# Mixture results returned to token order by row addresses, with a new order of norms and routes

## What is computed

```
# B, S, D = 2, 1024, 128; four blocks, each followed by a residual and a layernorm
x = _layernorm(x + attention(x))              # 16 heads of 64, q and k normalized
x = _layernorm(x + _moe_forward(x, ...))      # gate, top 2 of 8 experts
x = _layernorm(x + _L1_attn_ref(x, ...))      # depthwise convolution, then a recurrence
x = _layernorm(x + _L1_ffn_ref(x, ...))       # router, top 2 of 8 experts, one shared MLP
...
# first mixture, for the two chosen experts e of a token, weights by softmax of the two logits
hidden = silu(x_flat @ wge.T) * (x_flat @ wue.T);  out += we[:, None] * (hidden @ wde.T)
# recurrence, 16 states for each of 128 channels
dt = sigmoid(xf @ dt_w.T + dt_b) * (DT_MAX - DT_MIN) + DT_MIN
s = expA * s + (dtt * xt)[..., None] * b;  y = einsum('bcd,cd->bc', s, c)
# second mixture: two chosen experts, and the shared MLP for every token
_mlp(x) = square(relu(x @ w_fc.T)) @ w_proj.T
```

## Time and profile before

| | us |
|---|---|
| median of 3 runs | 1077.84 (1076.33 to 1078.65) |
| the profiled execution, its own time | 1075.24 |
| span of its profile | 1073.5 |

### The profile page before, as it was taken

One profiled execution on the slowest core, in us unless ns is written; L12 is line 12 of the kernel. 1 busy time (PEld: TensorE's weight loads), 2 busy tenths in 40 slices (PEclk: granted clock), 3 DMA queues, 4 the chain that ended last, 5 costly groups with the idle time before them and its releaser, 6 DMA issues. The chain is left out here.

```text
span 1073.5 us, 34731 instructions
## 1 busy us (share of the span) xinstructions
PE 913.9 (85%) x13676; PEld 858.4 (80%) x13676; DVE 728.1 (68%) x1463; ACT 770.0 (72%) x1275; POOL 501.1 (47%) x385
## 2 busy tenths in 40 slices
PE   4889999999999999999999951899969469899930
PEld 2778998999989989989999841899969359899830
DVE  6699988988998898889888744432459669410202
ACT  5689998988999889989988640544464266598831
POOL 5475755564655555555646116512328152043433
PEclk8799999999999999999999965899999689899975
DMA  8300000000000000000000041313201002023211
GB/s 263 113 2 6 18 3 22 3 3 22 3 3 22 3 22 3 3 23 3 2 22 2 2 177 38 103 54 86 54 26 30 3 28 70 11 68 97 61 55 42
DMA packets 43131, 42.13 MB, mean 39 GB/s; under 512 B 5600, under 2 KB 37344, under 8 KB 42848
## 3 DMA queue, kind: packets, MB, share of 16 engines
q1 hardware_dynamic: 38880, 31.51, 9.6%
q0 software_dynamic: 4096, 8.40, 2.7%
HBM read 25.60 MB, written 14.29 MB: 37 GB/s over the span
## 5 line engine op out<-in xcount | busy, mean ns | idle before, releaser
L557 ACT ACTIVATE Pr<-SC,cur_nesc,cur_esc 128x1024 f32<-128x1024 f32 x256 | 309.9, 1211 | 33.5 <-PE SC L417 17.0
L654 DVE TENSOR_TENSOR Pl<-Pr 128x1024 f16<-128x1024 f32 x224 | 287.5, 1302 | 44.8 <-ACT Pr L557 43.0
L416 PE MATMUL SC<-QK 128*128 128x256 f16 x1024 | 238.7, 274 | 1.0 <-ACT QK L539 1.0
L417 PE MATMUL SC<-QK 128*128 128x256 f16 x1024 | 238.6, 273 | 0.0
L442 PE MATMUL OP<-V,Pr 128*128 128x65 f16 x2048 | 214.4, 192 | 5.8 <-DVE Ob L676 5.7
L444 PE MATMUL OP<-V,Pr 128*128 128x64 f16 x2048 | 215.2, 195 | 0.0
L446 PE MATMUL OP<-V,Pl 128*128 128x65 f16 x2048 | 214.0, 191 | 0.0
L442 PEld LDWEIGHTS OP<-V,Pr 128*128 128x128 bf16 x2048 | 191.0, 97 | 12.5 <-issue 8.2
L444 PEld LDWEIGHTS OP<-V,Pr 128*128 128x128 bf16 x2048 | 190.0, 97 | 2.5
L446 PEld LDWEIGHTS OP<-V,Pl 128*128 128x128 f16 x2048 | 190.7, 99 | 0.0
L789 POOL TENSOR_TENSOR stk<-nrm,stk 128x512 f16<-128x512 f32 x64 | 75.2, 1175 | 147.6 <-DVE stk L636 147.6
(11 more groups left out here) (191 smaller groups left out, 2178.8 us busy)
## 6 DMA issues: line engine op xcount, KB each, us to landing
ys<-yb SPq DMA_DIRECT2D x92, 64.0 KB, 1.5
...
wd<-in_wd SPq DMA_DIRECT2D x4, 576.0 KB, 10.7
...
```

Source lines behind the costliest of these rows:

```text
L416: eng.matmul(out, QK[:, b, 1, key:key + P], rhs, start=True, stop=False)
L417: mm = eng.matmul(out, QK[:, b, 2, key:key + P], rhs, start=False, stop=True)
L557: eng.activation(Pr[:, n % PB, :, :], SC[s % 2][:, :, :], ACT.Exp, bias=cur_nesc[:, b:b + 1], scale=cur_esc[:, b:b + 1]).then_inc(s_exps, 1)
L654: eng.tensor_tensor(Pl[:, n % PB, :, :].rearrange("p a b -> p (a b)"), pr, high(pr)[:, 1::2], ALU.subtract).then_inc(s_low_probs, 1)
```

## The change

**Addresses.** A row of xs is now 288 f16 values long, 576 bytes. Behind the two halves stand the token's number plus 1024 and its first choice. xs and ys now exist once for each phase. At the start SP clears four tensors xs, not two, each with two DMAs, and the padding rows get addresses behind the results. When a chunk is loaded, two small DVE instructions (`return_addresses`) work out where each row's result belongs. The results go back by indirect DMA from POOL, one for each tile (`give_back`, 92 in all), straight to the place of token and choice. SP's 92 stores and POOL's 64 gathers are gone; SP reads a phase's results with four plain loads (`load_rows`). yb has 12 buffers.

**Waits.** `scatter` no longer waits for tiles: 16 DMAs go in a row. The third scatter stands ahead of phase 2's returns, the fourth behind the sixteenth return of phase 2.

**Order.** `place` follows `choose`, and ranks(0) stands ahead of logits(1). The norm, turn and convolution of batch 0 and its step products are spread over units 35 to 43, its tanh and first exponential stand at unit 45. The sums and the norm (1, 1) of phase 1 stand between the first 16 scans. The second batch's convolution is ahead of its route. Its states go through PE one per unit from unit 46, its last norm and turn are at units 64 and 65, the ranks at 69.

```diff
+        eng.wait_ge(self.s_zero, 4)
+        self.clear_rows(eng, range(B))
+
+    def clear_rows(self, eng, phases):
+        t = self.t
+        for ph in phases:
+            rows = t["xs"][ph].rearrange("(j p) c -> p j c", p=P)
+            eng.dma_start(rows[:, :, 0:2 * D],
+                          self.zero[:, :].unsqueeze(1).to_broadcast([P, TILES, 2 * D])).then_inc(self.s_cleared, 16)
+            eng.dma_start(rows[:, :, 2 * D:ROW], self.pad[:, :, :].bitcast(F16)).then_inc(self.s_cleared, 16)
...
                 eng.dma_start(wst[:, :], io["up0"][:, bass.ds(2 * FF * i, 2 * FF)]).then_inc(s_up_loaded, 16)
 
-            for i in range(H // 2):
+            load(0)
+            constants.sync(eng)
+            load(1)
+            constants.clear_rows(eng, range(B, 2 * B))
+            for i in range(2, H // 2):
                 load(i)
+            constants.sync_ended(eng)
 
...
 SORTED = TILES * P
+ROW = 2 * D + 32
+ADDRESS = slice(2 * D, 2 * D + 4)
 LAG2 = 2
...
-YR = 8
+YR = 12
...
+STEP_0 = CONVOLVE_0 + 1
 AHEAD = 10
-TURN_2 = SPARSE_2 + 5
+ROWS_2 = SPARSE_2 + 10
+TURN_2 = SPARSE_2 + 11
+RANKS_3 = TURN_2 + 4
 
 
 def states_behind(u):
 
-    n = AHEAD + 2 * (u - SPARSE_2)
-    return range(n, n + 2) if AHEAD <= n < DS else ()
+    n = AHEAD + u - SPARSE_2
+    return range(n, n + 1) if AHEAD <= n < DS else ()
 
 
 def sorted_tile(u):
...
                 wait(eng, s_sorted_turned, J - TILES + js.stop)
-                rows = xs[ph % 2].rearrange("(j p) c -> p j c", p=P)
+                wait(eng, s_dest, CHUNKS * (ph - 1) + c + 1)
+                rows = xs[ph].rearrange("(j p) c -> p j c", p=P)
                 eng.dma_start(xg[:, js, :], rows[:, js, :]).then_inc(s_sorted_loaded[c], 16)
 
-            def store(ph, j):
-                J = TILES * ph + j
-                eng.wait_ge(s_down_read, J + 1)
-                eng.dma_start(ys[ph % 2][P * j:P * j + P, :], yb[:, J % YR, :]).then_inc(s_y_stored[J % YR], 16)
+            def load_rows(ph, h):
+
+                for r in range(YR):
+                    wait(eng, s_y_stored[r], 16 * len(range(r, TILES * ph + TILES, YR)))
+                wait(eng, s_combined, 2 * TB * ph)
+                rows = ys[ph][0:2 * S].rearrange("(k i p) d -> p k i d", k=2, p=P)
+                for k in range(2):
+                    eng.dma_start(yg[:, k, 4 * h:4 * h + 4, :], rows[:, k, 4 * h:4 * h + 4, :]).then_inc(
+                        s_gathered[ph][h], 16)
 
             def store_out(b):
...
-                load(2, c)
-            for j in range(TILES):
-                store(2, j)
-            for c in range(CHUNKS):
-                load(3, c)
-            for j in range(TILES):
-                store(3, j)
+            for l in range(2):
+                for b in range(B):
+                    for c in range(CHUNKS):
+                        load(2 * l + b, c)
+                for b in range(B):
+                    for h in range(2):
+                        load_rows(2 * l + b, h)
             for b in range(B):
                 store_out(b)
             eng.wait_ge(s_out, 16 * 2 * B)
...
-                    turn(1, 0)
-            step_products(0)
+                if u in (TURN_1, TURN_1 + 1):
+                    turn(1, 0, (u - TURN_1,))
+                if u == STEP_0:
+                    step_products(0)
             for n in range(DS):
                 state_products(0, n)
+                if n == 12:
+                    turn(1, 1)
             turn(2, 0)
             logits(2)
-            turn(1, 1)
+            step_products(1)
             ranks(2)
             for u in range(SHARED_0, SPARSE_2 + LAG2):
                 if u < SPARSE_2:
                     up_products(u)
                 if u >= SHARED_0 + LAG2:
                     down_products(u - LAG2)
-                if u == STEP_1:
-                    step_products(1)
-                if u >= SPARSE_2 - 3:
...
-                if u == TURN_1:
-                    read(1, 0)
-            sigmoids(0)
-            for n in range(DS):
+                if u in (ROWS_1, ROWS_1 + 1):
+                    rows(1, 0, (u - ROWS_1,))
+                if u in (TURN_1, TURN_1 + 1):
+                    read(1, 0, (u - TURN_1,))
+                if u == SHARED_0 - 1:
+                    sigmoids(0)
+                    decays(0, 0)
+            for n in range(1, DS):
                 decays(0, n)
+                if n == 13:
+                    rows(1, 1)
+            read(1, 1)
             rows(2, 0)
             read(2, 0)
-            rows(1, 1)
-            read(1, 1)
             split_high(2)
             weights(2)
+            sigmoids(1)
+            decays(1, 0)
+            decays(1, 1)
             for u in range(SHARED_0, SPARSE_2):
                 activate(u)
...
@@ -1380,11 +1419,12 @@
                 for n in states_behind(u):
                     if n + NEA < DS:
                         decays(1, n + NEA)
+                if u == ROWS_2:
+                    rows(2, 1)
                 if u == TURN_2:
-                    rows(2, 1)
                     read(2, 1)
                     split_high(3)
-                if u == TURN_2 + 1:
+                if u == RANKS_3:
                     weights(3)
...
@@ -1498,6 +1539,19 @@
                 eng.tensor_tensor(w1l[m // 2][:, half], stage[:, n * m:n * m + n], w1h[m // 2][:, half],
                                   ALU.subtract).then_inc(s_w1_low, 1)
 
+            def return_addresses(ph, c):
+
+                b, js = ph % 2, chunk_tiles(c)
+                eng.wait_ge(s_sorted_loaded[c], 16 * ph + 16)
+                eng.tensor_tensor(is_first[:, js], sender[:, js, 1], owner[:, b, js], ALU.is_equal).then_inc(
+                    s_is_first, 1)
+                eng.wait_ge(s_is_first, CHUNKS * ph + c + 1)
+
+                wait(eng, s_y_stored[(TILES * (ph - 1) - 1) % YR],
+                     16 * len(range((TILES * (ph - 1) - 1) % YR, TILES * (ph - 1), YR)) if ph > 1 else 0)
+                eng.scalar_tensor_tensor(out=dest[:, b, js], in0=is_first[:, js], scalar=-float(S),
+                                         in1=sender[:, js, 0], op0=ALU.mult, op1=ALU.add).then_inc(s_dest, 1)
+
             def diagonal(n):
                 eng.tensor_scalar(diag[:, n, :], t["ident32"][:, :], t["bc"][:, n:n + 1], None, ALU.mult).then_inc(
                     s_diag, 1)
...
-                    statistics(1, 0, (0,))
-                if u == 40:
-                    combine(0, 1)
-                    statistics(1, 0, (1,))
-                if u == 41:
+                if u % TILES in RETURN_AT:
+                    return_addresses(u // TILES, RETURN_AT.index(u % TILES))
+                if u in (COMBINE_0, COMBINE_0 + 1):
+                    combine(0, u - COMBINE_0)
+                    statistics(1, 0, (u - COMBINE_0,))
+                if u == COMBINE_0 + 2:
                     shifts(1, 0)
-            convolve(0)
+                if u == CONVOLVE_0:
+                    convolve(0)
             step_inputs(0)
             for n in range(DS):
                 scan(0, n)
+                if n in (7, 9):
+                    combine(1, (n - 7) // 2)
+                    statistics(1, 1, ((n - 7) // 2,))
+                if n == 10:
+                    shifts(1, 1)
             add_states(0)
             statistics(2, 0)
-            combine(1, 0)
-            statistics(1, 1, (0,))
             shifts(2, 0)
-            combine(1, 1)
-            statistics(1, 1, (1,))
+            convolve(1)
+            split_low(2)
             choose(2)
-            shifts(1, 1)
             low(0)
-            split_low(2)
+            place(2)
             probabilities(2)
-            place(2)
-            convolve(1)
-            add_shared(SHARED_0)
-            add_shared(SHARED_0 + 1)
             step_inputs(1)
             for n in range(DS):
                 scan(1, n)
-                if n < TB - 2:
-                    add_shared(SHARED_0 + 2 + n)
+                if 0 <= n - 2 < TB:
+                    add_shared(SHARED_0 + n - 2)
+                if n in RETURN_2_AT:
+                    return_addresses(2, RETURN_2_AT.index(n))
             add_states(1)
             statistics(2, 1)
             shifts(2, 1)
+            split_low(3)
             choose(3)
-            split_low(3)
+            place(3)
             probabilities(3)
...
-            def scatter(ph, first=None):
+            def scatter(ph, pieces=range(2 * TB)):
 
                 b = ph % 2
-                eng.wait_ge(s_slots, ph + 1)
-                eng.wait_ge(s_split_low, ph + 1)
-                for k in range(2):
-                    for i in range(TB):
-                        if first is not None:
-
-                            wait(eng, s_gate_products, first + TB * k + i)
-                        eng.indirect_dma_start(
-                            out=xs[b], out_offset=bass.IndirectOffsetOnAxis(ap=slots[:, b, k, i:i + 1], axis=0),
```

(50 more changed lines are left out.)

155 lines of the change are left out of this document (83 added, 72 removed).

## The result

The changed kernel took 1097.85 us (median of four runs, 1092.64 to 1100.98) against 1077.78 (1076.33 to 1078.65) for the kernel before: a ratio of 1.0178, 95% interval 1.0146 to 1.0211. It is slower, where 1067.1 and "faster" had been forecast. Its profiled execution took 1092.64 us with a span of 1090.7. The same kernel was then measured again on two chips, and took **1058.57 us on one and 1096.81 on the other**. So there are two questions: what a chip of the second kind does, and what the change is worth without it. The table answers both at once: it cuts the spans at the same events. "First measurement" is the execution of 1092.64 us, "other chip" the profiled one of the fast chip, 1058.01 us (span 1056.0). The predicted column is worked out from the prediction's own times.

A forecast was written before the change was run, and what follows sets the result against it. PE bounds the first mixture's tile loop, DVE the scans, with serial passages between. Phase 3's start at +3.8 and the tail's -14.5 give -10.7: execution 1064.5, plus 2.6 to the runs' median, 1067.1 us; range 1058 to 1074.

The forecast's parts named there:

- Step 2: Into the first scans: step products, tanh and exponential move earlier, returns hide; first scan at 795.4, -4.9 us so far.
- step 7: Fourth scatter, behind tile 15's return: PE waits 5.8 to 5.9 us for unit 85's chunk, clock +2.3; phase 3 starts +3.8.
- rival C: POOL paces the tiles: at 2.18 us per return, phase 3 takes 8.5 longer, fourth scatter 5.9 later; 1081.5 us, chance 0.06.
- Step 1: First route: ranks ahead of logits(1) start the scatter 2.9 us earlier, at 646.9; longer rows cost the load +0.4; PE -2.5.
- Step 3: Between the scans: two sums with statistics at 3.5 us each, second exponential +0.8; norm rows of (2, 0) at 844.5, -0.2.
- Step 4: Third scatter: norm rows of (1, 1), turn and split are done before it, so it starts at 859.8, -6.4 us.
- Step 5: Second states on PE: 3.42 us per unit, offset reads +4.2, lower clock +2.5; phase 2's first turn at 901.6, -3.8.
- Steps 6 and 7: Phase 2's turn takes 8.4 us instead of 9.0 (-4.4 in all); then the fourth scatter's wait and clock give +3.8.
- Step 8: Tail: plain loads replace 16 gathers; first sum at 1040.5, second at 1044.0, -14.5 us on what ends last; norm and store stay.

The follow-up runs named there:

- g1_long_again: Changed kernel with fourth scatter behind tile 10's return, POOL pauses ahead of second and fourth scatters' DMAs and first three mixtures' returns; 1068.37 us (0.9904).
- d1_rows_before: Kernel before, with second scatter's waits removed (32 in a row) and fourth scatter 16 in a row from unit 66's product; 1110.11 us (1.0294).
- a4_pause3: Changed kernel with a one-column power on POOL as a pause ahead of each DMA of the fourth scatter alone; 1067.52 us (0.9916).
- f2_short_pause: Changed kernel with fourth scatter behind tile 10's return and a one-column memset ahead of scatter and return DMAs, leaving their distance at 1.28 us; 1049.45 us (0.9760).

## Why the prediction was wrong

**The missing term.** Steps 2 and 7 costed POOL's row of 32 scatters and its row of 16 by one thing, how late POOL itself would be, and found that this hides. That was right: POOL was not late, and its returns (0.96 to 1.44 us, 2.4 apart) paced no tile, so rival C's mechanism did not occur either. **What failed in steps 2 and 7 is the tacit premise under both steps that an indirect DMA issued beside tiles costs the other engines nothing.** On an S chip it costs them 18.8 us in the first mixture (two stops, the second beside six late returns from 784 to 792) and 16.5 net beside the fourth scatter. There the stop even covers the wait for the chunk that step 7 had forecast. No rival held this. Rival C came nearest in what it looked at, the rate of indirect DMAs, but asked whether POOL could keep up and not who else pays. The rule of the Trainium skill that stood beside it ("SBUF — State Buffer", section "Who interferes with whom") was used there for VectorE holding up GpSimd's descriptors. Its section lets either of the two hold up the other, but no third engine; here PE and ACT are held as well.

**Could the profile of before have told it?** Hardly. Most of its rows stand where PE had nothing to do: the first scatter, the last gather. Beside tiles nearly all its indirect DMAs wait for a gate product, but not all. Four gathers go in a row beside tiles, and so do eight DMAs of the third scatter (869.93 to 878.83, where PE also waits for sums):

```profile
740.14 0.99 POOL L1684 DMA_INDIRECT yg<-ys,slots  x1 [35.31 <-DMA ys<-yb]
741.43 0.95 POOL L1684 DMA_INDIRECT yg<-ys,slots  x1 [0.30 <-issue]
...
743.94 0.95 POOL L1684 DMA_INDIRECT yg<-ys,slots  x1 [0.30 <-issue]
```

PE is busy for 14.00 of the 14 us from 736 to 750 there. So the profile even seems to say that such a row is harmless; but four is fewer than the six that a stop took in `g1_long_again`, and the chip of this profile isn't recorded. On an S chip (`d1_rows_before`) even these gathers leave a small trace, at the fourth:

```profile
757.31 1.15 PE L1174 MATMUL DB<-wd,hid 128*128 x8 [1.00 <-ACT yb L1315]
```

What the prediction could have seen is that a row of 16 or 32 beside tiles stood nowhere in the trace: the edit took waits away where the kernel had hardly been seen without them. The rule of bounding what a trace does not show was applied to the load and the offsets, not to this.

**The steps on an N chip,** where the terms can be weighed one by one. The total is -17.5 against -10.7, and all the signs but one are right.

- Step 1: the first scatter as forecast (647.15, of 646.9). The chunk's load with 576-byte rows takes 4.21 us against 3.27 (4.12 in the first measurement), +0.9 where I took +0.4, and the first turn is 1.0 late (673.43). The count of beats in the Trainium skill ("DMA: Bandwidth & Descriptors", section "How a descriptor splits into AXI transactions"), which gave an estimate of +1.0, was nearer than mine by bytes.
- Step 2: first scan at 796.05 (795.4). Right.
- Step 3: +6.2 instead of +4.7. The sums with statistics took 3.36 us each, of 3.5 forecast, so it isn't they. The second scan starts 1.6 late instead of 0.8 (799.96), and the shifts of (1, 1), which the step had left out, stand among the scans and wait for a power of POOL that takes 2.95 us beside scans (1.0 us, 828.59 to 829.62).
- Step 4: -6.5, of -6.2. Right.
- Step 5: this is the mis-sized one, 5.0 us too dear. Units with states do take 3.4 us, but the reads of the experts' offsets (+4.2) left no gap: they ran under matmuls. The prediction had named 0 as their lower end, and took the upper. The clock cost about 1.8 of the 2.5 forecast.
- Steps 6 and 7: together +5.2 of +5.3, and the wait is the one forecast, released by the chunk's load. That the sum fits is partly luck, since two errors cancel: PE comes to unit 85 some 1.4 us earlier than forecast (970.67, 72.25 behind the turn of unit 54), and waits 1.4 longer. Behind the wait PE's granted clock is 0.55 in 978 to 983, against 1.00 before, and the last mixture takes 1.7 longer, of 2.3. On the other chip, the last scatter and the turn:

```profile
971.48 0.95 POOL L1725 DMA_INDIRECT xs<-split,slots  x1 [0.30 <-issue]
```

```profile
977.93 0.40 PE L1137 MATMUL XB<-ident,xg 128*128 128x128 f16 x2 [7.26 <-DMA xg<-xs]
```

The wait is 7.26 us of 5.9: the longer load explains about 0.5, and 0.9 comes from the fact that, against the forecast, PE is ready for the chunk 4.8 us earlier and the last scatter only 3.9. `a4_pause3` and `f2_short_pause` confirm the mechanism from both sides: +9.0 us for a last scatter 8.6 later, and -7.4 to -9.1 for one 9.3 earlier.

- Step 8: the first sum stands 7.1 us behind the last copy (forecast about 6; the load of the results took 3.34 us instead of 2.4) and the second 3.4 behind it, against 23.9 for the second before:

```profile
1041.72 2.19 DVE x L1584 x8
```

That is -13.4 of -14.5. The program's end, which I had left as it was, then comes 4.1 us sooner behind the last powers of POOL (7.4 instead of 11.5); why is not settled.

So the forecast time of 1067.1 us was 8.5 above what an N chip gives, with mechanisms that are right in the main, and 31 below what an S chip gives, for want of one.
